# An RWKV block and a cross-attention block in one kernel: group norm and gate taken per quarter, a front with second buffers, waits by chunk, and the bonus sum in four column groups

## The chip, the core and the metric

The kernel runs on one core of a Trainium2 chip. The core has TensorE (PE), VectorE (DVE), ScalarE (ACT), GpSimd (POOL) and SyncE (SP), and 16 DMA engines. The metric is the device time of one execution in microseconds (us); lower is better. All data is float32, and a float32 matmul shows in the trace as two passes, so its counts are twice those of the code.

## The reference

The input `x` is 16 batches of 128 positions by 512 channels; `ctx` has the same shape.

```python
# block 0 (RWKV, state = ctx), H = 32 heads of S = 16
xa = layer_norm(x); sx = previous position of xa - xa
xxx = tanh((xa + sx * maa_x) @ maa_w1)            # five low-rank parts of 32
xk, xw, xv, xr, xg = xa + sx * (maa_stack[j] + xxx[j] @ maa_w2[j])
w = exp(-exp(time_decay + tanh(xw @ td_w1) @ td_w2))
r, k, v = xr @ Wr.T, xk @ Wk.T, xv @ Wv.T;  g = silu(xg @ Wg.T)
for t: a = k_t v_t^T;  out_t = r_t (u * a + s);  s = a + w_t * s
og = group_norm(out) per head * gn_w + gn_b       # mean, variance over the 16 of a head
x1 = x + (og * g) @ Wo.T
xc = layer_norm(x1), shifted and mixed again
x2 = x1 + sigmoid(xr2 @ Wfr.T) * (relu(xk2 @ Wfk.T)**2 @ Wfv.T)
# block 1: instance norms of x2 and ctx, 1x1 convolutions, softmax attention, residual add
```

The term with `u` is called the bonus here: for one position it is `sum_i(r_i * u_i * k_i)` of a head, times `v`.

## The kernel before, in words

The 16 batches go in four quarters of four batches. Each engine runs its own program, and in each the order of the work is a string written out by hand (`ORDER_PE`, `ORDER_DVE` and so on), which says how many steps of which stream come next. An engine executes strictly in that order. The streams are:

- **a** (and **p**): the first stage, by quarter. Load x, layer norm, four turns (transposes) on PE, `EXT` (the normed input with one more column for the shift), `SX` (the difference), `first_mix` into `M1`, the low-rank product and tanh, copies of its rows by DMA (LT<-LE), then five mixes in the order v, w, k, r, g. A mix is two pairs of PE products (L1381) into two PSUM banks, for each of four chunks a `scalar_tensor_tensor` in PSUM (L1033) and an add into `M1` or `M2` (L1030). **p** projects the mixes (L1318), copies the result into `STG` (L778) and stores it in DRAM. The v parts are stored by five DMAs a chunk from ACT's queue (L786, L788). The gate g is `tanh` on ACT and a multiply on DVE (`gate`), and is stored too.
- **scan**: 64 steps, four a batch. SP loads 1 MB of v rows into `VB` (L499), POOL multiplies twice and adds once (L695, L699, L704), ACT writes two start columns (L847, L849) and the decays (L853), DVE runs the recurrence (L1150) and multiplies by r (L1030 on VB), and PE sums over channels in four column groups of 32 (L1440).
- **end**, once a batch: PE sums the bonus (L1454) with the 128-column weights `HEADU` and `HEAD`, DVE adds it to the scan's sum in `OT`; ACT squares `OT`, PE sums the squares (L1462), ACT copies the variance into `GV` (L878), POOL finds its inverse root in 13 small instructions (`newton`) and spreads it into `GS` (L716), PE broadcasts it (L1467), DVE multiplies `OT` by it, SP stores it.
- **c**: the rest of block 0 by quarter. ACT scales by `gn_w` and adds `gn_b` (`affine`, L884), DVE multiplies by the gate (`gated`), then four products of 16 matmuls each (wo, fk, fr, fv), layer norm, turns and mixes.
- **l, l1, l2, l3**: the attention of block 1 in four lanes of batches.

PE waits as whole tiles: `project` waits until all four chunks of a mix are added, `turn_a` until all four batches are normed. Streams a and c share `EXT`, `SX`, `M1`, `M2` and `XN`.

```python
def project(q, f, m):
    w.wait_ge(v_mad, 20 * q + 4 * (f + 1))
def shift_a(q):
    w.wait_ge(v_mad, 20 * q)
def first_mix(q):
    w.wait_ge(p_prj, 20 * (q - 1) + 16 if q else 0)
```

## Time and profile before

| | |
|---|---|
| median of 3 runs | 1023.35 us (1020.78 to 1023.88) |
| the profiled execution | 1016.36 us, its span 1014.6 us |
| busy in the span | PE 896.1, DVE 691.5, POOL 536.5, ACT 396.5 us |
| mean granted clock of PE | 0.936 of full speed |
| first and last scan sum (L1440) | 144.5 and 777.0 us |

A busy engine is not always an engine at full speed: where the granted clock is below 1, PE's passes take up to twice as long. An idle time matters only where nothing else could have ended the kernel later.

### The profile page before, as it was taken

The page shows a single profiled execution, that of the slowest core. Times are in us where ns is not written, and L with a number is a line of the kernel's source. Part 1 is how long each engine was busy: PE and PEld are TensorE (multiplying, and loading weights), DVE is VectorE, ACT ScalarE, POOL GpSimd, SP SyncE. Part 2 cuts the span into 40 slices and gives each one's busy share as a digit, 9 for nine tenths or more (in the row PEclk, how much of TensorE's full clock was granted, in tenths as well). Part 3 has the DMA queues.
Part 4 walks back from the last instruction along what each step waited for, and adds up shares of the span by engine and source line. Part 5 has one row for each costly group of instructions (what it writes and reads, how often), then busy time and mean ns, then how long its engine had stood idle before and what let it go on. Part 6 is the DMA issues. An engine that isn't in the chain of part 4 may idle for free.

```text
span 1014.6 us, 10745 instructions
## 1 busy us (share of the span) xinstructions
PE 896.1 (88%) x3588; PEld 398.5 (39%) x3588; DVE 691.5 (68%) x907; ACT 396.5 (39%) x819; POOL 536.5 (53%) x573
## 2 busy tenths in 40 slices
PE   1679978799786899688998999899998999979998
PEld 1233433343322343243343444344443454444454
DVE  6234499789988687888887698988998224442342
ACT  2013412333212241133223254565355554465395
POOL 2000388669987749648886778889682101000010
PEclk9687997899977899698999999999999999999999
DMA  7351679969689877878979844779642022001001
GB/s 270 134 125 73 179 178 222 233 171 233 162 187 216 209 184 196 212 145 224 243 182 281 216 112 100 183 192 227 163 99 83 21 73 83 21 4 39 21 0 42
DMA packets 100089, 150.69 MB, mean 149 GB/s; under 512 B 22850, under 2 KB 64066, under 8 KB 91842
## 3 DMA queue, kind: packets, MB, share of 16 engines
q1 hardware_dynamic: 73410, 129.03, 50.4%
q10 hardware_dynamic: 26624, 20.98, 8.5%
q8 instruction: 28, 0.46, 0.2%
q14 instruction: 27, 0.22, 0.1%
HBM read 115.38 MB, written 33.55 MB: 147 GB/s over the span
## 4 chain that ended last, share of the span: by engine, by line
PE 59%; DVE 14%; POOL 12%; issue 6%; ACT 5%; ACTq 2%; DMA 2%; SPq 0%; POOLq 0%; DVEq 0%
PE PS L1318 38%; PE PS L1381 4%; PE PS L1543 4%; POOL VB L704 4%; PE PS L1440 3%; PE PS L1520 2%; DVE PS L1033 2%; PE PS L1325 2%; POOL VB L699 2%; DVE VB L1150 2%; DVE M L1030 2%; DVE VB L1030 2%; POOL VB L695 2%; DVE M L1033 2%; PE PS L1454 1%
## 5 line engine op out<-in xcount | busy, mean ns | idle before, releaser
L1318 PE MATMUL PS<-M,W 128*128 128x512 f32 x672 | 329.8, 634 | 23.7 <-DVE M L1033 12.3
L1318 PEld LDWEIGHTS PS<-M,W 128*128 128x128 f32 x672 | 128.7, 202 | 198.2 <-issue 167.5
L704 POOL TENSOR_TENSOR VB<-VB 128x1024 f32<-128x1024 f32 x64 | 151.4, 2366 | 58.9 <-ACT VB L849 56.2
L1150 DVE TENSOR_TENSOR_SCAN VB<-PS,VB 128x512 f32<-128x512 f32 x128 | 149.1, 1206 | 25.9 <-POOL VB L704 17.3
L587 POOL TENSOR_SCALAR NM<-MV 128x2 f32<-128x2 f32 (+1 forms) x24 | 6.2, 258 | 283.7 <-DVE MV L1278 183.0
L1030 DVE TENSOR_TENSOR VB<-VB,PS 128x2048 f32<-128x2048 f32 x64 | 145.9, 2280 | 1.5
L695 POOL TENSOR_TENSOR VB<-KR,VB 128x1008 f32<-128x1008 f32 x64 | 129.7, 2026 | 17.5 <-DMA VB<-scr_vs 17.5
L699 POOL TENSOR_TENSOR VB<-WG,VB 128x1008 f32<-128x1008 f32 x64 | 129.3, 2020 | 0.0
L1033 DVE SCALAR_TENSOR_TENSOR PS<-PS,VEC,SX 128x512 f32<-128x512 f32 x80 | 60.2, 752 | 87.7 <-PE PS L1381 72.4
L1318 PE MATMUL PS<-W,M 128*128 128x512 f32 x224 | 105.1, 595 | 0.0
L1296 DVE TENSOR_REDUCE SM<-PS 128x1 f32<-128x512 f32 x64 | 44.0, 688 | 58.9 <-PE PS L1543 58.4
L1440 PE MATMUL PS<-VB,HEAD 128*32 128x512 f32 x512 | 72.5, 643 | 12.3 <-DVE VB L1030 7.0
L778 ACT ACTIVATE STG<-PS 128x512 f32<-128x512 f32 x48 | 28.5, 594 | 122.3 <-PE PS L1318 110.6
L1381 PE MATMUL PS<-LE,W 32*128 32x512 f32 x64 | 47.7, 834 | 29.0 <-DVE M L1030 21.1
L853 ACT ACTIVATE PS<-WP 128x512 f32<-128x512 f32 x64 | 38.3, 598 | 80.4 <-DVE VB L1150 74.1
L1318 PE MATMUL PS<-W,SX 128*128 128x512 f32 x128 | 61.1, 597 | 0.0
L1543 PE MATMUL PS<-LS 128*128 128x512 f32 x112 | 58.6, 617 | 1.6 <-ACT LE L973 1.6
L1318 PEld LDWEIGHTS PS<-W,M 128*128 128x128 f32 x224 | 40.5, 190 | 44.0 <-issue 43.2
L1030 DVE TENSOR_TENSOR M<-PS,EXT 128x512 f32<-128x512 f32 x80 | 55.2, 690 | 2.3
L973 ACT ACTIVATE LE<-PS,SM 128x512 f32<-128x512 f32 x44 | 30.1, 684 | 53.1 <-DVE SM L1296 53.1
L1381 PE MATMUL PS<-LT,W 32*128 32x512 f32 x64 | 48.2, 841 | 0.0
L1033 DVE SCALAR_TENSOR_TENSOR LS<-PS,WOB,X 128x512 f32<-128x512 f32 x14 | 10.4, 748 | 46.0 <-PE PS L1318 46.0
(167 smaller groups left out, 1280.5 us busy)
## 6 DMA issues: line engine op xcount, KB each, us to landing
VB<-scr_vs SPq DMA_DIRECT2D x64, 1024.0 KB, 7.9
W<-in_w SPq DMA_DIRECT2D x8, 1024.0 KB, 9.8
X<-in_x SPq DMA_DIRECT2D x4, 1024.0 KB, 8.2
scr_vs<-STG ACTq DMA_DIRECT2D x64, 64.0 KB, 5.7
scr_v<-STG ACTq DMA_DIRECT2D x16, 256.0 KB, 6.9
scr_w<-STG ACTq DMA_DIRECT2D x16, 256.0 KB, 8.3
scr_k<-STG ACTq DMA_DIRECT2D x16, 256.0 KB, 2.7
KR<-scr_k SPq DMA_DIRECT2D x16, 256.0 KB, 8.1
```

The source lines that it names most:

```text
L695: po.tensor_tensor(vo, KO[:, 0:N2 - 1].unsqueeze(1).to_broadcast([P, S, N2 - 1]), vo, ALU.mult).then_inc(g_kv, 1)
L699: po.tensor_tensor(ve, KE[:, 0:N2 - 1].unsqueeze(1).to_broadcast([P, S, N2 - 1]), ve, ALU.mult).then_inc(g_kv, 1)
L704: po.tensor_tensor(flat(bv[:, 0]), flat(bv[:, 0]), flat(bv[:, 1]), ALU.add).then_inc(g_kv, 1)
L853: ac.activation(PS[:, 5, :].rearrange("p (j n) -> p j n", n=N2), WP[:, bb % 2, m].unsqueeze(1).to_broadcast([P, 8, N2]), ACT.Copy).then_in ...
L1030: return dv.tensor_tensor(o, a, b, op)
L1033: return dv.scalar_tensor_tensor(out=o, in0=a, scalar=s, in1=b, op0=op0, op1=op1)
L1150: sc = dv.tensor_tensor_scan(s_, PS[:, 5, :], b_, 0.0, ALU.mult, ALU.add)
L1296: dv.reduce_max(SM[:, cs, tc, 0:1], PS[:, BANK_L[bb, ("sc", tc)], :], AX_X, negate=True).then_inc(vb[ln], 1)
L1318: mm = pe.matmul(o, l, r, start=i == 0, stop=i == 3)
L1381: mm = pe.matmul(PS[:, ns[i], :], W2[DM * g:DM * g + DM, 2 * i + j, :], low_rank(f, i), start=True, stop=True)
L1440: mm = pe.matmul(PS[32 * g:32 * g + 32, 4, :], HEAD[:, m, 0], VB[:, k % NB, :, 4 * g:4 * g + 4].rearrange("p s j n -> p j s n"), start=m = ...
L1543: pe.matmul(PS[:, n, :], X[:, 2, tc * P:(tc + 1) * P], X[:, 3, :], start=True, stop=True).then_inc(pb[ln], 1)
```

## The change

1. **Norm and gate by quarter.** Squares, variance, inverse root and scaling leave stream `end` and are done once a quarter at the head of stream `c`. The inverse root works on 128 columns, four times, instead of on 32 columns, 16 times. `affine` and `gated` go; DVE's new `normed` does 12 instructions a quarter. The gate is stored as half the projection (an ACT copy), and its tanh and product come in stream c.
2. **Bonus in four column groups.** 32 small matmuls a batch with 32-column weights, four ACT copies into the block-diagonal `DG`, one matmul that broadcasts 192 columns.
3. **Front ahead.** Odd quarters have their own `EXT` and `SX` (in space of `LL` and `LS`), and the front is a stream of its own beside the mixes (stream `m`). In the first quarter the mixes of v, w and k have four PSUM banks instead of two.
4. **Waits by chunk.** PE waits for each chunk or pair of chunks just before the matmul that reads it. The add of a mix takes two chunks at once (but for g).
5. **Queues.** The v stores go from ACT's queue to SP's. ACT's second start column goes; POOL's add leaves the first column out.
6. All five order strings are new.

```diff
-                    for wt, cols in ((HEADU, slice(0, L)), (HEAD, slice(L, L + N2))):
+                    w.wait_ge(a_dg, 4 * bb)
+                    w.wait_ge(v_ot, 4 * bb - 1 if bb else 0)
+                    for wt, at, n, to in ((HEADU, 0, 32, 192), (HEAD, L, 16, 224)):
                         for m in range(C4):
-                            mm = pe.matmul(PS[:, 7, cols], flat(wt[:, m]), RQ[:, m, cols], start=m == 0,
-                                           stop=m == C4 - 1)
+                            for g in range(4):
+                                mm = pe.matmul(PS[H * g:H * g + H, 7, to:to + n], wt[:, m],
+                                               RQ[:, m, at + n * g:at + n * g + n], start=m == 0, stop=m == C4 - 1)
                     mm.then_inc(p_end, 1)
...
+                    w.wait_ge(a_dg, 4 * (bb + 1))
+                    pe.matmul(PS[:, 7, 0:192], SAME[:].rearrange("p g h -> p (g h)"), flat(DG[:]), start=True,
                               stop=True).then_inc(p_end, 1)
...
             def stream_c():
                 for q in range(NQ):
+                    w.wait_ge(a_sq, 4 * (q + 1))
+                    n = banks.take(w, BANK_C[q, "var"], a_gv, q + 1)
+                    for c in range(C4):
+                        for b in range(QB):
+                            mm = pe.matmul(PS[H * b:H * b + H, n, 0:L], SAME[:, 0], SQ(q)[:, c, b * L:(b + 1) * L],
+                                           start=c == 0, stop=c == C4 - 1)
+                    mm.then_inc(p_gn, 1)
+                    w.wait_ge(g_gn, 14 * (q + 1))
+                    pe.matmul(PS[:, n, :], SAME[:].rearrange("p g h -> p (g h)"), SQ(q)[:, 0, :], start=True,
+                              stop=True).then_inc(p_gn, 1)
...
+            def norm_gate(q):
+                for m in range(4):
+                    w.wait_ge(d_og, 16 * (q + 1))
+                    w.wait_ge(v_mad, 10 * NQ)
+                    w.wait_ge(p_fr, 4 * q)
+                    ac.activation(SQ(q)[:, m, :], OG(q)[:, m, :], ACT.Square).then_inc(a_sq, 1)
...
+                ac.activation(GV[:], PS[:, n, 0:L], ACT.Identity, bias=EB[:]).then_inc(a_gv, 1)
+                for m in range(4):
+                    ac.activation(SQ(q)[:, m, :], XN[:, m, :], ACT.Tanh).then_inc(a_gate, 1)
...
+            def normed(q):
+                for m in range(4):
+                    w.wait_ge(p_gn, 2 * q + 2)
+                    stt(O[:, m, :], O[:, m, :], vec(V_GNW + m), PS[:, n, :], ALU.mult, ALU.mult).then_inc(v_scl, 1)
+                for m in range(4):
+                    stt(G[:, m, :], G[:, m, :], 1.0, XN[:, m, :], ALU.add, ALU.mult).then_inc(v_gate, 1)
+                    stt(O[:, m, :], O[:, m, :], vec(V_GNB + m), G[:, m, :], ALU.add, ALU.mult).then_inc(v_y, 1)
...
+            def stream_n():
+                for q in range(NQ):
+                    w.wait_ge(a_gv, q + 1)
+                    yield from newton(GR[:], GV[:], GT[:], g_gn, 14 * q)
+                    po.tensor_tensor(btv(SQ(q)[:, 0, :]), GR[:].unsqueeze(1).to_broadcast([P, 4, L]),
+                                     MASK[:].unsqueeze(2).to_broadcast([P, 4, L]), ALU.mult).then_inc(g_gn, 1)
...
+        EXTS = [EXT[:], LL[:, 3 * E:3 * E + C4 * QB * (L + 1)].rearrange("p (c b t) -> p c b t", c=C4, b=QB)]
+        SXS = [SX[:], LS[:, 1]]
...
-                w.wait_ge(v_mad, 20 * q)
-                yield from shift(v_sub)
+                w.wait_ge(v_mad, 10 * (q - 1))
+                yield from shift(v_sub, q % 2)
...
-                w.wait_ge(v_mad, 20 * q + 4 * (f + 1))
...
+                yield from four_mm(PS[:, n, :], [(W[:, wi, ec, m * P:(m + 1) * P], M[:, ec, :]) for ec in range(C4)], p_prj,
+                                   (w, v_mad, 10 * q + 2 * f, 2))
...
+            def store_v(q, m):
+                w.wait_ge(a_cp, 12 * q + m + 1)
+                for g in range(4):
+                    sp.dma_start(vs_late[q, m, g], rows).then_inc(d_vs[m], 16)
+                sp.dma_start(dr["v"][q, m], STG[:, ss, :]).then_inc(d_st_["v"][m], 16)
...
-                    w.wait_ge(a_s0, 2 * k + 2)
-                    po.tensor_tensor(flat(bv[:, 0]), flat(bv[:, 0]), flat(bv[:, 1]), ALU.add).then_inc(g_kv, 1)
+                    po.tensor_tensor(vo, vo, ve, ALU.add).then_inc(g_kv, 1)
...
-                    w.wait_ge(p_end, 3 * bb + 3)
-                    tt(OT[:], OT[:], PS[:, 7, 3 * L:4 * L].unsqueeze(1).to_broadcast([P, C4, L]), ALU.mult).then_inc(v_ot, 1)
```

## Rows read from the trace of the kernel before

**Rows 1.** The page: busy time of the engines; shares of the last chain

```profile
PE 896.1 (88%) x3588; PEld 398.5 (39%) x3588; DVE 691.5 (68%) x907; ACT 396.5 (39%) x819; POOL 536.5 (53%) x573
...
PE 59%; DVE 14%; POOL 12%; issue 6%; ACT 5%; ACTq 2%; DMA 2%; SPq 0%; POOLq 0%; DVEq 0%
```

**Rows 2.** Busy time by stretch: PE, weight loads, DVE, ACT, POOL, clock, DMA

```profile
0.00:90.00 90.00, 53.99 (x149) 22.37 (x150) 37.31 (x54) 18.00 (x31) 6.53 (x26) 0.79 0.53 161
90.00:200.00 110.00, 93.83 (x359) 39.70 (x358) 79.10 (x93) 30.62 (x65) 65.31 (x52) 0.92 0.79 190
200.00:600.00 400.00, 354.54 (x1559) 148.33 (x1557) 328.93 (x373) 118.68 (x266) 301.36 (x286) 0.91 0.80 197
600.00:777.00 177.00, 169.35 (x786) 78.79 (x786) 158.47 (x204) 95.96 (x203) 145.82 (x156) 0.99 0.66 162
777.00:1014.60 237.60, 224.35 (x746) 109.33 (x738) 87.71 (x187) 133.28 (x257) 17.51 (x55) 0.99 0.12 33
```

**Rows 3.** What PE waited for in the first 90 us: total, times, longest

```profile
PE PS L1325 <- ACT XN L745: 15.4, 1, 15.4
PE PS L1318 <- DVE M L1033: 6.0, 1, 6.0
PE PS L1381 <- DVE M L1030: 5.2, 3, 3.1
PE PS L1381 <- ACT STG L802: 4.2, 1, 4.2
```

**Rows 4.** What PE waited for from 200 to 600 us

```profile
PE PS L1381 <- DVE M L1030: 12.2, 6, 3.4
PE PS L1440 <- DVE VB L1030: 7.0, 4, 4.4
```

**Rows 5.** PE's timeline, 570 to 600 us: start, duration, instructions

```profile
577.59 1.05 PE L1454 MATMUL PS<-RQ,HEADU 128*128 128x128 f32 x8
...
579.32 3.65 PE L1318 MATMUL PS<-W,M 128*128 128x512 f32 x8
...
589.13 0.46 PE L1462 MATMUL PS<-KR,SAME 128*32 128x32 f32 x32
589.52 1.98 PE L1318 MATMUL PS<-W,SX 128*128 128x512 f32 x4
...
597.44 1.07 PE L1440 MATMUL PS<-VB,HEAD 128*32 128x512 f32 x8
```

**Rows 6.** DVE's groups: busy, mean ns, idle before and its releasers

```profile
L1033 DVE SCALAR_TENSOR_TENSOR PS<-PS,VEC,SX 128x512 f32<-128x512 f32 x80 | 60.2, 752 | 87.7 <-PE PS L1381 72.4 <-PE PS L1362 13.3 <-PE PS L1318 2.0
L1030 DVE TENSOR_TENSOR M<-PS,EXT 128x512 f32<-128x512 f32 x80 | 55.2, 690 | 2.3
...
L1030 DVE TENSOR_TENSOR OT<-OT,PS 128x512 f32<-128x512 f32 x32 | 21.7, 679 | 6.7 <-PE PS L1440 4.0 <-PE PS L1467 2.5
L1033 DVE SCALAR_TENSOR_TENSOR STG<-STG,PS 128x512 f32<-128x512 f32 x32 | 21.7, 678 | 18.3 <-PE PS L1318 18.3
L1030 DVE TENSOR_TENSOR SX<-EXT 128x1024 f32<-128x1024 f32 x16 | 19.8, 1273 | 17.3 <-ACT EXT L754 12.0 <-ACT EXT L903 5.2
```

**Rows 7.** POOL's groups

```profile
L704 POOL TENSOR_TENSOR VB<-VB 128x1024 f32<-128x1024 f32 x64 | 151.4, 2366 | 58.9 <-ACT VB L849 56.2
...
L610 POOL TENSOR_TENSOR GT<-GT,GV 128x32 f32<-128x32 f32 x48 | 15.0, 313 | 2.9
...
L716 POOL TENSOR_TENSOR GS<-GR,MASK 128x128 f32<-128x128 f32 x16 | 7.3, 455 | 1.4
...
L602 POOL TENSOR_SCALAR GR<-GV 128x32 int32<-128x32 int32 x16 | 4.3, 268 | 37.6 <-ACT GV L878 37.0
```

**Rows 8.** ACT's timeline, 53 to 56 us, its DMA issues

```profile
53.03 2.64 ACTq L786 DMA_DIRECT2D scr_vs<-STG  x4
55.70 0.62 ACTq L788 DMA_DIRECT2D scr_v<-STG  x1
```

**Rows 9.** ACT's groups

```profile
L849 ACT ACTIVATE VB<-S 128x16 f32<-128x16 f32 x64 | 14.2, 221 | 2.8 <-ACT STG L778 1.5 <-issue 0.8 <-ACT STG L828 0.4
...
L873 ACT ACTIVATE KR<-OT 128x512 f32<-128x512 f32 x16 | 10.0, 625 | 24.7 <-DVE OT L1030 24.7
```

**Rows 10.** What SP's queue waited for

```profile
SPq L499 <- PE PS L1440: 316.5, 52, 18.4
```

More of the change, by code:

```diff
@@ L177 @@
 BANK_A.update({t: 2 + i % 2 for i, t in enumerate(TAKES_P)})
-TAKES_C = [("wo", b) for b in range(4)] + [("tr", ec) for ec in range(4)] + [("fk", f) for f in range(4)]
+for _t in TAKES_A:
+    if _t[0] == "mix":
+        BANK_A[_t] = _t[3] % 2 + (6 if _t[1] == 0 and _t[2] < 3 and _t[3] // 2 else 0)
+TAKES_C = [("var",), ("rstd",)] + [("wo", b) for b in range(4)] + [("tr", ec) for ec in range(4)] + [("fk", f) for f in range(4)]
 TAKES_C += [(n, b) for b in range(4) for n in ("fr", "fv")]
@@ L817, in stream_p @@
                         yield
-                        yield from store(NAMES[0], q, m)
+                    hs, n = slot(("t", q)), BANK_A["td1", q]
+                    w.wait_ge(p_td1, q + 1)
+                    ac.activation(STG[:, hs, 0:NT // 2], PS[:, n, 0:NT // 2], ACT.Tanh).then_inc(a_td, 1)
+                    yield
                     for m in range(4):
@@ L887, in stream_c @@
             def stream_c():
-                for m in range(C4):
-                    affine(0, m)
-                    yield
                 for q in range(NQ):
+                    yield from norm_gate(q)
                     w.wait_ge(g_stc, 4 * (q + 1))
@@ new lines, in stream_a, with stream_m @@
+            def stream_a():
+                for q in range(NQ):
+                    for b in range(QB):
+                        stats_a(q, b)
+                        yield
+                    yield from sums_a(q)
+                    if q == 0:
+                        yield from centre_wv()
+                    yield from shift_a(q)
+                    yield from first_mix(q)
+            def stream_m():
+                for q in range(NQ):
+                    for f in range(5):
+                        yield from mix(q, f)
@@ L1418, in stream_a, with stream_m @@
                         yield from low_a(q, part)
+            def stream_m():
+                for q in range(NQ):
                     for f in range(5):
```

370 lines of the change are left out of this document (171 added, 199 removed), and 170 rows, old and new, of tables (ORDER_ACT, ORDER_DVE, ORDER_PE, ORDER_POOL).

## The prediction

> **What bounds the kernel now.** I read the page first, for the busy shares and the chain that ended last, then PE's, DVE's and POOL's busy time by stretch, then what PE waited for in each stretch, then the groups of each engine for the durations.
>
> PE is busy for 896.1 us of 1014.6, and the last chain runs through it for 59%; DVE has 14% and POOL 12% [rows 1]. But part of the busy time is at a lowered clock. Busy time times what the clock lacks of 1 is 0.21 x 54.0 = 11 us up to 90 us, 0.08 x 93.8 = 8 up to 200, 0.09 x 354.5 = 32 up to 600, and 4 after that, 55 us in all [rows 2]. At full clock PE's work is thus some 896 - 55 = 841 us. The other 1016 - 841 = 175 us of the profiled execution are 118 us of idle PE (36.0, 16.2, 45.5, 7.7 and 13.2 in the five stretches, span minus busy) and those 55; 2 us lie around the span. After 600 us little is left to win; before it, about 98 us of idle and 51 of clock stand [rows 2].
>
> Why is PE idle there? At the start, because the first stage is one serial line: 15.4 us until the first normed tiles, 6.0 for `first_mix`, 5.2 for mix adds that hold both banks, 4.2 for a tanh [rows 3]. From 200 to 600 us, because DVE comes late with adds (12.2) and scan products (7.0) [rows 4], and DVE and POOL are themselves 82% and 75% busy there [rows 2]. POOL's own chain has waits in it that are not work: 56.2 us for ACT's second start column before its add, and 37.0 us for the variance [rows 7].
>
> **The change part by part, PE.** The bonus took 577.59 to 579.32, so 1.73 us a batch for 16 passes; the sum of squares 0.39 us for 32 passes of 32 columns in four groups [rows 5]. The new bonus is 32 passes of 32 columns and 32 of 16. Nothing of 16 columns is in the trace; I take the price of the 32-column ones, 0.39, since they can hardly cost more, and the low bound is half of it. That is 0.8 us. The broadcast grows from 128 to 192 columns, by 0.1 us or so (a 512-column pass is 3.65/8 = 0.46 at most [rows 5]). Per batch 1.73 + 0.39 go and 0.8 + 0.1 come: 1.2 saved, 19 us over 16 batches. Per quarter come 32 passes of 128 columns in four groups, the same columns as one scan sum, 1.07 us [rows 5], and one broadcast of 512 columns, 0.9: 8 us over four. PE's work falls by about 11 us. If small passes would not run side by side, 64 of them at 1.73/16 = 0.11 us are 7 us a batch, so the other bound is +80 us; the row at 589.13 speaks against it, with 12 ns a pass.
>
> The Trainium skill says in "TensorEngine Tiling (Array Packing)", section Instruction Overhead, that a matmul costs about 60 cycles however few columns it has, and warns against taking the tiling factor from a dimension that is already small. By that page 64 passes are an estimated 64 x 25 ns = 1.6 us and the bonus would save almost nothing, so the forecast would be some 13 us higher. The 32 passes in 0.39 us [rows 5] do not fit a price paid one after the other, so I go by the row.
>
> **POOL.** The inverse root took 4.3 + 7.3 us plus four kinds of 48 instructions at about 0.3 us (one row of the four stands), 69 us in all [rows 7]. On 128 columns one instruction should take up to 0.46, as L716 does; the spread to 512 columns lies between that and the 2.37 of 1024, say 1.3. A quarter is 13 x 0.45 + 1.3 = 7 us, all 28. So 40 us of work go, with the 37 us wait in the middle of the scan work, and the 56.2 us wait for ACT goes wholly. POOL's add itself I leave at 2.3. Off the path this is worth nothing; its worth is in the scan products that DVE delivers earlier.
>
> **DVE.** Out go 16 gate products, 16 scalings of `OT` (0.68 each) and 16 `gated`, in come 48 `scalar_tensor_tensor`s at 0.68 to 0.75 [rows 6]: nothing saved, but 32 of them move from the mixes and scans to stream c. 64 adds of 0.69 become 32 double ones; the nearest row is the 1024-element subtraction at 1.27 [rows 6], so 44.2 becomes 41, bounds 38 and 44. It is 3 us.
>
> **ACT and SP.** ACT loses 64 start columns of 0.22, gains 64 copies into `DG` of about the same (0.22, up to 0.3), and the squares (0.625 [rows 9]) only move. What matters is issue time: four v stores took 2.64 us and the fifth 0.62 [rows 8], over 3 us a chunk, 16 chunks, so 52 us leave ACT for SP. The 4.2 us wait for the decay's tanh [rows 3] stood behind such issues and goes. On SP they are queued between loads that wait for scan sums, 316.5 us in 52 waits, 6 us each, at most 18.4 [rows 10]. What is behind such a wait is a v store, and behind that the `STG` slot and ACT's next copy.
>
> **The front.** Of the first 36 us of idle PE I count off 2 to 3 of the 15.4 (transposes follow the norms one by one, and run beside them), 2 of the 6.0, the 5.2 (four banks), 3 for v projections that now start after the first pair, 4.2 for the tanh, and of the 11 us of lowered clock a third, since the clock here follows idle stretches: 20 us, of which I take 15, because the first chain stays serial in its dependences. The second `EXT` and `SX` free the turns and the shift of the next quarter, but `first_mix` still waits until r of the quarter before is projected, as `M1` is single. So the lead is the four projections of g, 16 matmuls of 0.9 or 14 us, and no quarter. From 90 to 200 us I take 8 of 16.2 + 8 us.
>
> **The middle.** From 200 to 600 us idle and clock cost 45.5 + 32 = 77 us. With POOL's waits gone, DVE relieved of 22 us, waits by chunk and the early front, I take just under half, 35. This is the largest term and a judgement: its bounds are 0 (DVE, 82% busy, keeps its pace) and 65.
>
> **What it adds.** Each quarter of stream c now begins with a chain: four squares 2.5, sum 1.1, copy 0.3, inverse root 7, broadcast 0.9, 12 DVE instructions 9, together 21 us, where affine and gated took about 4, woven into the quarter before. It can't begin before the last fr product of the quarter before, since the squares lie in `M2`. That is 17 us more a quarter. While it runs, PE has the attention of the quarter before: from its shapes about 15 columns-of-512 matmuls a batch, 13 us, 52 us a quarter. So it is hidden but for rough edges, 5 us. If the cover is gone it costs 68.
>
> **Sum.** -11 (PE) -15 (front) -8 -35 (middle) +5 = -64, so 1016.4 becomes 952 us in the profiled execution. The median of the runs shown is 7 us above the profiled one; I predict 958 us.
>
> **Rivals.**
> - *Middle at DVE's pace.* The scans still leave DVE no earlier, as it is busy for 328.9 of the 400 us there [rows 2] and its work is unchanged. Then the term of 35 is 0 to 10: 985 us. For it speaks that DVE's share even rises to 158.5 of 177 us after 600 us [rows 2]; against it that DVE's waits are on POOL and PE. The same time comes if v stores sit behind waiting loads on SP (6 waits of 6 us) or if the front's lead is cut by `M1`.
> - *Everything fits.* Middle gives 65: 925 us. PE's 830 us of work plus 25 at the start and 20 at the end would even allow 875, so it is not excluded.
> - *Slower: the norm chain is not covered.* POOL works in order, and its inverse root stands among the scan multiplies; if its input is late, the multiplies behind it wait, then DVE, then PE. The price is the 17 us a quarter and the 7 us that POOL stands in it, 24 or 96 in all, against 69 gained elsewhere: 1023 - 69 + 96 = 1050 us. It decides from the third quarter on in which PE has nothing else in its order during the chain (72 us); in one or two it takes 24 to 48 back.
> - *The column groups don't run side by side.* Plus 80 us, which also ends above 1023. The row of 0.39 us makes it unlikely.
>
> **How the numbers follow.** Forecast with its own range 940 to 975: 0.52. Everything fits: 0.15. Middle at DVE's pace or SP: 0.20, 975 to 1010. No change, within 0.3% (3 us, about what a measurement can tell): 0.04. Slower: 0.09 (chain 0.07, groups 0.02). Below 920 or above 1005 I leave about 0.05 and 0.15, so the range is 918 to 1003. Faster has 0.52 + 0.15 + 0.20 = 0.87.
>
> **What would show it.** In the profile after, PE's busy time should be near 850 or less with a clock of 0.96 or more; PE's idle time before 90 us some 20 instead of 36. L1454's successor should show 64 small passes in about 0.8 us a batch. POOL's idle time before its add should be near nothing, its inverse root 56 instructions at 0.4 to 0.5. The last scan sum should stand at about 710 instead of 777 us. It is wrong if PE waits for `normed` more than 10 us in all, if SP's waits lengthen the copies from `STG`, or if DVE is busy over 92% until the last scan with PE idle beside it.

## The result, and the profile of the kernel after

The changed kernel takes 1046.6 us (1043.3 to 1047.2, 4 runs) against 1023.6 beside it: a ratio of 1.022 [1.020, 1.025], 23 us slower, where 958 us were forecast. The profiled execution took 1046.2 us. Times here and below are medians and ratios are of means, both of undisturbed executions: one of the four of e5 took 4896 us and is left out.

The page of the kernel after, busy times and the shares of the last chain, as in [rows 1]:

```profile
PE 898.5 (86%) x3980; PEld 387.1 (37%) x3980; DVE 708.1 (68%) x875; ACT 394.1 (38%) x807; POOL 505.6 (48%) x403
...
PE 63%; DVE 17%; issue 5%; DMA 5%; ACT 4%; POOL 3%; SPq 2%; ACTq 0%; DVEq 0%; POOLq 0%
```

Busy time by stretch of the kernel after, columns as in [rows 2]:

```profile
0.00:90.00 90.00, 62.93 (x174) 26.57 (x175) 41.25 (x57) 21.26 (x33) 6.54 (x26) 0.89 0.60 170
90.00:200.00 110.00, 94.89 (x422) 35.47 (x421) 80.48 (x82) 28.54 (x64) 66.00 (x38) 0.86 0.85 195
200.00:600.00 400.00, 331.44 (x1640) 130.77 (x1640) 314.49 (x315) 104.95 (x228) 270.24 (x164) 0.88 0.77 189
600.00:777.00 177.00, 160.10 (x839) 71.92 (x838) 151.40 (x192) 87.18 (x185) 122.95 (x105) 0.96 0.64 155
777.00:1044.40 267.40, 249.10 (x911) 122.36 (x909) 120.45 (x231) 152.19 (x297) 39.90 (x72) 0.98 0.15 41
```

Read as in the prediction: what PE's busy time lacks of full clock is 0.11 x 62.9 + 0.14 x 94.9 + 0.12 x 331.4 + 0.04 x 160.1 + 0.02 x 249.1 = 71 us, so its work at full clock is 898.5 - 71 = 827 us, 14 less than before. The work fell as forecast. The rest of the span grew: idle PE is 146 us (27.1, 15.1, 68.6, 16.9, 18.3) instead of 118, the clock's share 71 instead of 55. Most of it is the stretch from 200 to 600 us, 68.6 + 40 against 45.5 + 32 in [rows 2]; after 600 us idle and clock together cost 47 us instead of 25.

What PE waited for in the kernel after, in the first 90 us (first two rows, beside [rows 3]) and from 200 to 600 us (beside [rows 4]):

```profile
PE PS L1341 <- ACT XN L762: 12.1, 4, 11.5
PE PS L1332 <- DVE M L1042: 5.3, 1, 5.3
```

```profile
PE PS L1399 <- DVE M L1039: 13.9, 8, 3.7
PE PS L1461 <- DVE VB L1039: 11.4, 5, 5.7
PE PS L1332 <- DVE M L1042: 10.9, 3, 4.7
PE PS L1332 <- DVE LS L1042: 10.6, 1, 10.6
```

The last row is new: Wo of quarter 0 waits for `normed`. The scan sums wait longer for DVE than before (11.4 against 7.0).

What POOL waited for in the kernel after (its waits for the last layer norms left out), beside the waits at the end of the lines of [rows 7]:

```profile
POOL VB L714 <- DMA VB<-scr_vs: 110.7, 23, 17.5
...
POOL NM L606 <- DVE MV L1249: 43.4, 4, 20.5
POOL WP L704 <- DMA WG<-scr_w: 27.3, 5, 11.3
POOL GR L621 <- ACT GV L893: 25.1, 4, 9.7
```

The wait for ACT's second start column is gone, as forecast. In its place stand 110.7 us of waits for the loads of `VB`, which took 17.5 us before.

The starts of VectorE's scans show where the time goes. Batch 8 starts at 421 us, 27 us *earlier* than before (448). Then the gap from batch 9 to 10 is 66 us (39 before), from 11 to 12 it is 70 (36), from 14 to 15 it is 54 (41), and the last scan sum stands at 846.5 us instead of 777.0. Each of these long gaps holds the norm and gate of a quarter. The first Wo result is added at 529.5 us, 20.6 later than before. The end comes only 30 us later although the last scan sum comes 69.5 later, because 198 us lie behind that sum now and 238 before.

### The profile page after: what moved, and what is told of

Read it like the earlier page. It is cut to its first block, busy times and chain, and to the rows that moved or that the text cites. A ratio compares the mean times of both kernels' runs of the same rounds, so it can differ in the third digit from the quotient of the medians.

```text
span 1044.4 us, 11193 instructions
## 1 busy us (share of the span) xinstructions
PE 898.5 (86%) x3980; PEld 387.1 (37%) x3980; DVE 708.1 (68%) x875; ACT 394.1 (38%) x807; POOL 505.6 (48%) x403
## 4 chain that ended last, share of the span: by engine, by line
PE 63%; DVE 17%; issue 5%; DMA 5%; ACT 4%; POOL 3%; SPq 2%; ACTq 0%; DVEq 0%; POOLq 0%
PE PS L1332 42%; PE PS L1576 5%; PE PS L1399 4%; DVE VB L1154 3%; PE PS L1461 3%; PE PS L1553 3%; PE PS L1341 3%; DVE VB L1039 3%; DVE PS L1042 2%; DVE M L1042 2%; DVE M L1039 2%; DMA scr_v<-STG 2%; DVE SX L1039 1%; PE PS L1544 1%; DVE LS L1042 1%
## 5 line engine op out<-in xcount | busy, mean ns | idle before, releaser
L1332 PE MATMUL PS<-M,W 128*128 128x512 f32 x672 | 338.9, 647 | 24.3 <-DVE M L1042 18.0
L714 POOL TENSOR_TENSOR VB<-KR,VB 128x1008 f32<-128x1008 f32 x64 | 131.2, 2049 | 110.7 <-DMA VB<-scr_vs 110.7
L722 POOL TENSOR_TENSOR VB<-VB 128x1008 f32<-128x1008 f32 x64 | 152.9, 2389 | 4.5
L718 POOL TENSOR_TENSOR VB<-WG,VB 128x1008 f32<-128x1008 f32 x64 | 131.5, 2054 | 0.0
L1461 PE MATMUL PS<-VB,HEAD 128*32 128x512 f32 x512 | 74.7, 665 | 13.0 <-DVE VB L1039 12.8
L1399 PE MATMUL PS<-LL,W 32*128 32x512 f32 x128 | 47.7, 839 | 24.2 <-DVE M L1039 19.5
L1042 DVE SCALAR_TENSOR_TENSOR PS<-PS,VEC,SX 128x512 f32<-128x512 f32 x40 | 28.9, 752 | 51.1 <-PE PS L1399 41.3
L982 ACT ACTIVATE LL<-PS,SM 128x512 f32<-128x512 f32 x44 | 30.1, 684 | 59.3 <-DVE SM L1307 59.2
L1042 DVE SCALAR_TENSOR_TENSOR PS<-PS,VEC,LS 128x512 f32<-128x512 f32 x40 | 29.1, 753 | 28.4 <-PE PS L1399 25.2
L1332 PE MATMUL PS<-LL,LS 128*128 128x512 f32 x88 | 41.5, 603 | 3.5 <-ACT LL L1028 3.5
L1341 PE MATMUL PS<-ID,XN 128*128 128x128 f32 x128 | 23.0, 299 | 21.1 <-ACT XN L762 12.1
```

The lines of the kernel that those rows point to most:

```text
L714: po.tensor_tensor(vo, KO[:, 0:N2 - 1].unsqueeze(1).to_broadcast([P, S, N2 - 1]), vo, ALU.mult).then_inc(g_kv, 1)
L718: po.tensor_tensor(ve, KE[:, 0:N2 - 1].unsqueeze(1).to_broadcast([P, S, N2 - 1]), ve, ALU.mult).then_inc(g_kv, 1)
L722: po.tensor_tensor(vo, vo, ve, ALU.add).then_inc(g_kv, 1)
L1042: return dv.scalar_tensor_tensor(out=o, in0=a, scalar=s, in1=b, op0=op0, op1=op1)
L1332: mm = pe.matmul(o, l, r, start=i == 0, stop=i == 3)
L1341: mm = pe.transpose(PS[:, n, i * P:(i + 1) * P], tile, ID[:])
```

## The experiments

Ratios are to the kernel before on the same chip; the changed kernel's own is 1.022 [1.020, 1.025]. The changed kernel was not run again on the chips of the experiments, where the kernel before took 1017 to 1020 us (median), and executions of one kernel there differ by up to 1.3% (e13: 1014.3 to 1027.9). So two ratios that differ by half a per cent or less are not told apart. "Last sum" is the start of the last scan sum in the kept trace: 846.5 us in the changed kernel, 777.0 before.

### Where v and g are stored, and the waits by pair

First theory (A): the v stores, now in SP's queue between loads, hold the loads. `e1_v_on_act` puts them back on ScalarE, `e3_vg_on_act` g as well, `e2_loads_between` keeps them on SP and moves loads ahead of them. `e4_whole_waits` undoes the wait by pairs of chunks in the projections.

```diff
# e1 (in copy_a's loop for v, ScalarE; SP's five issues a chunk go)
+                        ss = SLOT_STG["v", q, m]
+                        w.wait_ge(a_cp, 12 * q + m + 1)
+                        for g in range(4):
+                            rows = STG[32 * g:32 * g + 32, ss, :].rearrange("h (s n) -> h s n", n=N2)
+                            ac.dma_start(vs_late[q, m, g], rows).then_inc(d_vs[m], 16)
+                        ac.dma_start(dr["v"][q, m], STG[:, ss, :]).then_inc(d_st_["v"][m], 16)
# e4
-                                   (w, v_mad, 10 * q + 2 * f, 2))
+                                   (w, v_mad, 10 * q + 2 * f + 1, 4))
```

Expected of e1: 

> The changed kernel, but the five v stores of a chunk are issued from ACT's queue right behind the copy, and SP's steps for them do nothing. Theory A (the v stores on SP hold back the VB loads behind them, so POOL waits 110.7 us for VB<-scr_vs where it waited 17.5, and the last scan sum comes at 846 us instead of 777): POOL's wait for that DMA falls below 50 us, the last scan sum comes before 800 us, the time falls from 1046.6 to 990 to 1020 us. Theory B (the new orders, the norm chain and DVE's slow all-SBUF instructions cost it, the loads are only late because the scans are): the wait may move but the time stays within 8 us of 1046, or rises, as ACT gets 52 us of issue time back.

Expected of e2: 

> The changed kernel with SP's order alone altered: in the second, third and fourth quarter the next KR, WG and VB loads stand ahead of the burst of v stores or between its chunks; the stores stay on SP. Theory A: about half of what moving them to ACT gives, 1020 to 1035 us, since a load and a store still hold each other up in one queue. Theory B: no change, 1040 to 1050 us.

Expected of e3: 

> As the v stores on ACT, and the stores of the gate too, which stood on SP in the kernel before as well. SP waited 40.7 us in 7 times for the gate's copies in the changed kernel. Theory A: loads behind them come earlier, another 3 to 10 us below the run with the v stores alone. Rival: the gate's stores fall where no VB slot is free, and it is within 3 us of that run. Theory B: as for the first, no gain over 1046.

Expected of e4: 

> The changed kernel with one part undone: a projection waits for all four chunks of its mix before its first matmul instead of pair by pair. If the wait by chunk gives what I forecast (3 us at the start and part of the middle), this is 3 to 12 us slower than 1046.6. If waits by chunk do harm by stalling PE inside an open group, it is faster. If DVE's pace sets the mixes anyway, within 3 us.

Measured: e1 1062.1 us, 1.044 [1.040, 1.048]; e2 1094.1 us, 1.075 [1.070, 1.079]; e3 1059.7 us, 1.042 [1.039, 1.044]; e4 1058.8 us, 1.041 [1.038, 1.043]. Theory A fell: stores on SP are some 20 us better than on ScalarE. With the stores on ScalarE GpSimd still waits 115.6 us for the loads of `VB` (110.7 in the changed kernel, under 50 expected), and the last sum stands at 861.4 us. Letting loads pass the stores is worse still: in e2 ScalarE waits longer for the `STG` slots (49.4 us at L829 on scr_v, 21.8 in the changed kernel) and GpSimd longer for loads (150.2 us); which of the two makes the time was not tested. Undoing the waits by pair costs about 18 us, more than the 3 to 12 expected.

### The products of norm and gate beside GpSimd's multiplies

VectorE's timeline of the kernel after, `normed` of quarter 0 (start, duration, instructions), and then GpSimd's and TensorE's beside it:

```profile
506.38 2.73 DVE L1042 SCALAR_TENSOR_TENSOR LS<-LS,VEC,PS 128x512 f32<-128x512 f32 x4 [4.62 <-PE PS L1505]
509.02 0.69 DVE L1042 SCALAR_TENSOR_TENSOR LS<-LS,XN 128x512 f32<-128x512 f32 x1
509.74 2.72 DVE L1042 SCALAR_TENSOR_TENSOR LS<-LS,VEC 128x512 f32<-128x512 f32 x1
512.38 2.48 DVE L1042 SCALAR_TENSOR_TENSOR LS<-LS,XN 128x512 f32<-128x512 f32 x1
...
522.31 0.68 DVE L1042 SCALAR_TENSOR_TENSOR LS<-LS,XN 128x512 f32<-128x512 f32 x1
523.03 0.75 DVE L1042 SCALAR_TENSOR_TENSOR LS<-LS,VEC 128x512 f32<-128x512 f32 x1
```

```profile
506.90 2.00 POOL L718 TENSOR_TENSOR VB<-WG,VB 128x1008 f32<-128x1008 f32 x1
...
514.27 2.44 POOL L718 TENSOR_TENSOR VB<-WG,VB 128x1008 f32<-128x1008 f32 x1
...
541.74 0.23 POOL L606 TENSOR_SCALAR NM<-MV 128x4 f32<-128x4 f32 x1 [19.90 <-DVE MV L1249]
```

```profile
523.83 15.95 PE L1332 MATMUL PS<-W,LS 128*128 128x512 f32 x32 [10.55 <-DVE LS L1042]
```

The four products with an operand in PSUM take 0.68 us each. Those with both tensor operands in SBUF take 2.4 to 2.8 us as long as GpSimd multiplies beside them, and 0.68 to 0.75 once it stands (from 521.8 us on). One exception, the product at 509.02, began with GpSimd's add of 508.98: it took 0.69, and the add 2.92 instead of 2.39. GpSimd's multiplies go from 2.00 to 2.44 us in the same stretch. So `normed` took 17.4 us instead of 9, and PE stood 10.55 us for it.

The Trainium skill has the rule, in "SBUF — State Buffer", section Who interferes with whom: a VectorE instruction with two SBUF inputs contends with a GpSimd instruction that reads SBUF, and whichever comes first holds the shared port for its whole instruction. The trace agrees for VectorE: 0.7 us become 0.7 plus most of one GpSimd multiply of 2.0. GpSimd loses less, 0.44 us a multiply. The prediction did not weigh it, though the trace of the kernel before shows it: a product with both tensor operands in SBUF that takes 0.69 us as a rule took up to 2.81 there (min, median and max in ns):

```profile
L1033 DVE SCALAR_TENSOR_TENSOR X<-STG,X x16: 675/691/2814, 569.9 to 970.9; 128x512 f32<-128x512 f32 x16
```

Three runs tell the theories apart. `e5_psum_products` writes the tanh into PSUM and keeps the gate product there, in one bank, so that each tanh now waits for the product before it and no longer for the spread; `e6_no_products` leaves out the gate and the bias product; `e7_short_root` leaves out two Newton steps of three.

```diff
# e5
-                    w.wait_ge(p_gn, 2 * q + 2)
+                    w.wait_ge(a_gv, q + 1)
+                    w.wait_ge(v_y, 4 * q + m)
...
-                    ac.activation(SQ(q)[:, m, :], XN[:, m, :], ACT.Tanh).then_inc(a_gate, 1)
+                    ac.activation(PS[:, n, :], XN[:, m, :], ACT.Tanh).then_inc(a_gate, 1)
...
-                    stt(G[:, m, :], G[:, m, :], 1.0, XN[:, m, :], ALU.add, ALU.mult).then_inc(v_gate, 1)
+                    stt(G, G, 1.0, XN[:, m, :], ALU.add, ALU.mult).then_inc(v_gate, 1)   # G in PSUM
# e6: both products of a chunk
+                    dv.tensor_copy(O[:, m, 0:1], G[:, m, 0:1]).then_inc(v_y, 1)
# e7
-                for i in range(3):
+                for i in range(1):
```

Expected of e5: 

> The whole computation, but the gate's tanh is written to the PSUM bank that the mean square has left, and the gate product stays there, so that of the 12 products of a quarter none has all its operands in SBUF. Theory C (the chain of norm and gate is slow because VectorE's products with all operands in SBUF take 2.0 to 2.8 us beside GpSimd's scan multiplies instead of 0.7): each of the 8 falls to about 0.75 us, 10 to 13 us less for each quarter that lies in the scan stage, less some 4 us because one tanh now waits for the product before it; over three quarters 18 to 27 us, so 1020 to 1028 us and a ratio to the kernel before of 1.00. Theory D (the time is lost where GpSimd and VectorE, in order, stand at stream c's steps with the scans queued behind them, whatever the products cost): the products get short, but the scan's end moves by under 8 us, ratio 1.015 to 1.02.

Expected of e6: 

> Leaves out the gate product and the bias product (8 of the 12 of a quarter); a copy of one column takes the place of each pair. Upper bound of what the products cost. Theory C: 15 us a quarter on VectorE and on the way to the projection Wo, of which three quarters lie in the scan stage: 30 to 45 us, ratio 0.98 to 0.995. Theory D: under 12 us, ratio 1.01 or more.

Expected of e7: 

> Leaves out two of the three Newton steps of the inverse root (8 of 14 GpSimd instructions of a quarter, 0.3 to 0.5 us each, 3.8 us a quarter). If the chain square, sum, root, spread, products is uncovered (the rival of the prediction), each of the first three quarters gets 3.8 us shorter and GpSimd has as much more for the scan: 8 to 12 us less, ratio 1.011 to 1.014. If it is covered, nothing: ratio 1.022.

VectorE's timeline of e5 at the same place:

```profile
506.50 0.69 DVE L1043 SCALAR_TENSOR_TENSOR PS<-PS,XN 128x512 f32<-128x512 f32 x1
507.23 0.75 DVE L1043 SCALAR_TENSOR_TENSOR LS<-LS,VEC,PS 128x512 f32<-128x512 f32 x1
508.65 0.70 DVE L1043 SCALAR_TENSOR_TENSOR PS<-PS,XN 128x512 f32<-128x512 f32 x1 [0.67 <-ACT PS L899]
```

Every product is back at 0.69 to 0.75 us, and GpSimd's multiplies at 2.00, so the contention is shown as the cause of their length. `normed` takes 10.6 us instead of 17.4, PE's wait for it is gone, the first Wo result is added at 520.8 us instead of 529.5, and the last sum stands at 839.0. In its place PE waits 3.8 us for a copy that stands behind the tanhs in ScalarE's order. Yet e5 took 1045.2 us (1036.5 to 1046.9), 1.024 [1.017, 1.031]: nothing of the 10 us of idle PE can be seen at the end, though by the interval a gain of half a per cent is not excluded. e6 took 1020.9 us, 1.003 [1.000, 1.006], some 20 us less than the changed kernel, with the last sum at 820.6. e7 took 1035.3 us, 1.017 [1.012, 1.021], between the two answers expected of it. By theory C the run e5 should have come near e6; it did not. The length of the products is real, but only part of their price.

### The places where the queues stand

`e8_pool_scans_first`: GpSimd stood 19.9 us (521.8 to 541.7, row above) at the second layer norm of quarter 0 with scan multiplies queued behind; this run puts four scan steps ahead of it. `e9_squares_early`: ScalarE stood 12.0 us for the squares of quarter 0, whose buffer is now the second `SX` of the odd quarters; this run puts them elsewhere. `e10_chain_early` also moves mean, spread and root ahead in the orders; `e11_early_psum` adds e5 to that. `e12_scan_between` moves one scan sum, one load and three scan steps ahead of stream c's block.

```diff
# e8, GpSimd's order
-    n:2 scan:1 n:12 scan:9 c:4 scan:4 c:1 scan:8
+    n:2 scan:1 n:12 scan:13 c:5 scan:8
# e9, squares of quarter 0 by chunk into LE
-                    w.wait_ge(v_mad, 10 * NQ)
+                    if q:
+                        w.wait_ge(v_mad, 10 * NQ)
+                    else:
+                        w.wait_ge(p_mix, 10 * NQ - 2)
+                        w.wait_ge(p_sq, m - 1)
# e12, TensorE's order
-    c:49 l:8 scan:1 end:1
+    c:16 scan:1 c:33 l:8 end:1
```

Expected of e8: 

> Nothing is changed but GpSimd's order at one place: the four small instructions of the second layer norm of quarter 0, for which GpSimd waited 19.9 us (521.8 to 541.7) with scan multiplies behind them, go behind the next four scan steps. Theory D: about 9 us of scan work fill the wait, the scan's end comes 5 to 9 us sooner, ratio 1.013 to 1.017. Theory C: the scans gained wait for VectorE anyway, which is busy with the slow products and then waits for Wo; ratio 1.02 to 1.025.

Expected of e9: 

> The whole computation. Only the squares of quarter 0 go to another place (by chunk into two free rows of the first stage's low rank buffer) instead of LS, which the front of the odd quarters now uses as its second buffer; so ScalarE no longer waits 12.0 us (477.6 to 489.6) for the last double add of quarter 3 with its scan and project steps queued behind. No order is changed. Theory E (the second buffers hold the first norm chain and, through ScalarE's order, the scan): the 12 us go, part comes back as ScalarE's wait for TensorE's mean of squares, which stands later in TensorE's order; first use of Wo 3 to 6 us sooner, ratio to the kernel before 1.015 to 1.02. Rival (the wait is covered, since the chain waits for TensorE's order anyway): no change, 1.022 to 1.024.

Expected of e10: 

> As the kernel before this one, and three steps of the chain of quarter 0 stand earlier in the orders: TensorE's mean of squares ahead of the last two mixes of quarter 3, its spread where the mean stood, GpSimd's root ahead of two scan multiplies. Theory E: the chain square, mean, root, spread, products starts about 12 us sooner and its first use of Wo about 8 us sooner, 6 to 9 us less than the changed kernel: ratio 1.014 to 1.017. Rival: VectorE, with four scan steps ahead of the products, gives nothing of it on: 1.020 or more.

Expected of e11: 

> Both together: the earlier chain of quarter 0, and the gate's tanh and product in PSUM in all quarters, so that no product beside GpSimd's multiplies has all operands in SBUF. If the two causes add, Wo of quarter 0 starts 15 us sooner than in the changed kernel: ratio 1.005 to 1.012. If a third cause (scans held behind stream c's block on TensorE and on the queues) sets the end, 1.015 to 1.02.

Expected of e12: 

> Only orders: one scan step of TensorE goes from behind its block of 49 steps of stream c (fk, fr, fv of quarter 0, 562.3 to 605.2, whole 43 us) to behind the first 16 of them; one load of SyncE goes ahead of the stores and loads of stream c, and three scan steps of GpSimd ahead of the inverse root of quarter 1. The product that this scan sum reads was made at 567.7 and summed at 611.0; the next load stood until 612.1 and GpSimd and VectorE ran out of scan work. Theory F (in the changed kernel the scans starve behind TensorE's block, which keeps TensorE busy now and idle later): the gap between the scan starts of batches 11 and 12 falls from 70 us to 58 to 62, the last scan sum comes 8 to 12 us sooner, ratio 1.010 to 1.015. Rival (the later stages are paced by TensorE's own work, the scans only wait with it): the gap falls but the end stays, 1.020 to 1.024.

Measured: e8 1043.6 us, 1.023 [1.018, 1.029]; e9 1041.3 us, 1.024 [1.019, 1.029]; e10 1047.8 us, 1.030 [1.025, 1.035]; e11 1035.6 us, 1.019 [1.015, 1.023]; e12 1043.4 us, 1.026 [1.022, 1.030]. None of e8, e9 and e12 is faster than the changed kernel's 1.022, and e10 is slower (1.030). e11 differs from e10 by e5's products alone and is 1.1% faster, with intervals that do not meet: with the chain early, the length of the products does reach the end. Against the changed kernel e11's 1.019 is not told apart. The traces show what becomes of the time. First ScalarE's timeline at the squares, of the kernel after:

```profile
489.63 1.15 ACT L886 ACTIVATE LS<-LS 128x512 f32<-128x512 f32 x2 [12.00 <-DVE M L1039]
```

and of e9:

```profile
478.68 1.15 ACT L893 ACTIVATE LL<-LS 128x512 f32<-128x512 f32 x2 [7.41 <-DMA LS<-scr_o]
...
483.77 1.15 ACT L893 ACTIVATE LL<-LS 128x512 f32<-128x512 f32 x2 [3.45 <-PE PS L1507]
```

The wait for the double add is gone, and behind it stood two others, the load of o and PE's mean. In e10 the mean comes earlier still (copied at 478.5 us against 485.5 in e9), but VectorE then waits 12.4 us for TensorE before the last mixes, `normed` begins only at 503.3, and Wo of quarter 0 is added at 530.0 instead of e9's 523.2.

SyncE's timeline of the kernel after in the gap between batches 11 and 12:

```profile
565.42 0.64 SPq L518 DMA_DIRECT2D VB<-scr_vs  x1
589.24 0.32 SPq L427 DMA_DIRECT2D scr_g<-STG  x1
589.74 0.37 SPq L545 DMA_DIRECT2D XN<-scr_g  x1
590.21 0.52 SPq L549 DMA_DIRECT2D M<-scr_o  x1
612.13 0.52 SPq L518 DMA_DIRECT2D VB<-scr_vs  x1
```

No load of `VB` is issued for 46.7 us, because TensorE's 49 steps of stream c (busy from 562.3 to 605.2) stand ahead of the scan sum that frees a buffer. TensorE's timeline of e12 shows that sum moved, and the next one:

```profile
571.86 1.07 PE L1461 MATMUL PS<-VB,HEAD 128*32 128x512 f32 x8
...
610.66 3.53 PE L1461 MATMUL PS<-VB,HEAD 128*32 128x512 f32 x16
```

The gap of 70 us became 71, with the next sum now the one that stands. Theory F is refuted for a single step: moving one sum only made the next one the late one.

### Both kernels without norm and gate

The pair that decides. Both kernels lose norm and gate whole; a copy of one column stands for each output chunk, and every order, load and store stays.

```diff
# e13, changed kernel: squares, mean, root, spread, tanh and products go
+                for m in range(4):
+                    w.wait_ge(d_og, 16 * (q + 1))
+                    w.wait_ge(d_gl, 16 * (q + 1))
+                    dv.tensor_copy(O[:, m, 0:1], XN[:, m, 0:1]).then_inc(v_y, 1)
# e14, kernel before: squares, sum, root, spread, last product by batch, gate product, affine go
-                    mm.then_inc(p_end, 1)
+                    mm.then_inc(p_end, 3)
```

Expected of e13: 

> The changed kernel without the norm and the gate: no squares, mean, inverse root, spread, tanh or products; a copy of one column stands in for each output chunk, all orders, buffers, loads and stores stay. If theory G holds (the rest of the change gives what was forecast, 25 to 45 us, and the norm and gate by quarter cost far more than the 5 us of the forecast because they are not covered), this is far under the changed kernel, 970 to 995 us, a ratio to the kernel before of 0.955 to 0.975, and 20 us or more under the kernel before treated in the same way (next run). If theory H holds (the rest of the change loses too, by its orders and its longer in-order queues), it stands within 10 us of the kernel before treated in the same way.

Expected of e14: 

> The kernel before without its norm and gate: no square, sum, root, spread and last product by batch, no gate product in the projection, no affine step; a copy of one column for each output chunk. What it gives is the price of norm and gate in the kernel before. Both theories expect little, since GpSimd's roots and VectorE's products there lie beside TensorE's work: 15 to 30 us less than the kernel before, ratio 0.97 to 0.985. The difference to the run before this one is the worth of everything else in the change.

Measured: e13 1021.9 us, 1.004 [1.001, 1.007]; e14 1022.1 us, 1.002 [1.000, 1.005]. Theory H holds for the gain: without norm and gate the two kernels are equal within 0.2%, so all the rest of the change together, forecast at 69 us, is worth nothing. Norm and gate cost the changed kernel 1.8% (1.022 to 1.004), 18 us, and the kernel before nothing. e6 had that already (1.003): once eight products a quarter are gone, leaving out squares, mean, root, spread and tanh as well gives nothing more. These are prices by removal, and they do not add up: undoing the store queue (e1) or the waits by pair (e4) costs the changed kernel about 2% each, so if those hold without the norm too, something else in the change must lose about as much. The last sum hints at the order strings, 816.9 us in e13 against 783.8 in e14, but no run has the new orders alone.

Why leaving so much out gives the kernel before nothing is in its waits. GpSimd's waits from 100 to 500 us in e14:

```profile
POOL VB L704 <- ACT VB L841: 72.5, 12, 10.7
POOL VB L695 <- DMA VB<-scr_vs: 41.0, 12, 10.7
```

In the kernel before itself these two were 38.4 and 14.8 us there, and 26.4 us went to the variance. The root's 60 us of work and that wait are gone, and the time comes back as longer waits at the next two places. The changed kernel has for the same stretch:

```profile
POOL VB L714 <- DMA VB<-scr_vs: 82.5, 16, 17.5
```

The stretch from 200 to 600 us, first e13, then e14 (e13's kept trace is of its fastest execution, 1014.3 us, e14's of one of 1022.9):

```profile
200.00:600.00 400.00, 332.10 (x1724) 131.36 (x1722) 310.07 (x330) 111.13 (x244) 264.97 (x157) 0.92 0.80 194
```

```profile
200.00:600.00 400.00, 347.20 (x1212) 141.91 (x1210) 325.39 (x349) 104.55 (x235) 261.61 (x154) 0.90 0.78 194
```

Over the whole of e14's trace PE's work at full clock is 829 us, 12 less than before, and idle and lowered clock together 192 us, 18 more.

### Are the loads the pace?

`e17_after_half_loads` and `e18_before_half_loads` cut each `VB` load from the fifth on to its first half; the other half keeps what lay there.

```diff
+                        part = slice(0, S * L if k < NB else S * L // 2)
-                        sp.dma_start(VB[:, k % NB].rearrange("p s j n -> p (s j n)"), src).then_inc(d_vb[k % NB], 16)
+                        sp.dma_start(VB[:, k % NB].rearrange("p s j n -> p (s j n)")[:, part],
+                                     src[:, :, part]).then_inc(d_vb[k % NB], 16)
```

Expected of e17: 

> The changed kernel with every load of the scan's values from the fifth on cut to its first half (the other half of the buffer keeps what lay there); all instructions and waits stay. Theory L (with norm and gate gone from the scan stage and the start columns on ScalarE, the scan is paced by the round of the four buffers: a load of 9.7 us, then GpSimd's three multiplies, VectorE's scan and product, TensorE's sum, and only then the next load; GpSimd's waits for loads grew from 14.8 us to 82.5 us between 100 and 500 us): a load falls to 5 to 6 us, about 4 us less in a round of four chunks, 1 us a chunk, 30 to 60 us less over the scan, ratio to the kernel before 0.965 to 0.99. Rival (TensorE's and VectorE's own order sets the pace and GpSimd's waits for loads are slack): under 10 us, ratio 1.012 or more.

Expected of e18: 

> The same cut of the loads in the kernel before. There GpSimd waits only 14.8 us for loads between 100 and 500 us, so by theory L it gains less than the changed kernel: 0 to 15 us, ratio 0.985 to 1.0. If it gains as much as the changed kernel does, the loads were its pace too, and the change had nothing to win in GpSimd's other waits. If neither gains, the round of the buffers is no bound in either.

Measured: e17 1054.8 us, 1.035 [1.031, 1.039]; e18 1013.4 us, 0.994 [0.992, 0.996]. A load fell from 9.7 to 5.5 us in e17 and from 7.9 to about 5.2 in e18, but theory L fell: with loads half as long the kernel before gains 0.6%, and the changed one loses 1.2%. GpSimd's wait for loads in e17 is still 60.0 us between 100 and 500. The last sum moved 9 us later in e17. A part of the loss may lie in the products. VectorE's groups in `normed` of quarter 1 (600 to 650 us), of the kernel after and then of e17:

```profile
L1042 DVE SCALAR_TENSOR_TENSOR M<-M,VEC 128x512 f32<-128x512 f32 x4 | 6.2, 1560 | 0.1
L1042 DVE SCALAR_TENSOR_TENSOR M<-M,XN 128x512 f32<-128x512 f32 x4 | 4.4, 1106 | 0.9 <-ACT M L898 0.9
```

```profile
L1044 DVE SCALAR_TENSOR_TENSOR M<-M,XN 128x512 f32<-128x512 f32 x4 | 9.2, 2303 | 0.0
L1044 DVE SCALAR_TENSOR_TENSOR M<-M,VEC 128x512 f32<-128x512 f32 x4 | 8.5, 2129 | 0.1
```

In the changed kernel GpSimd stood 2.4 and 1.2 us for loads within this `normed`, in e17 0.6 us in all, and the eight products take 17.7 us instead of 10.6. That these 7 us reach the end is not shown (e5's did not), and the other 6 us were not traced.

### Attempts at a better version

`e15_psum_root2` has e5's products, e9's squares and two Newton steps; `e16_psum_pow` has one power instruction for the whole root.

```diff
# e16
-                    yield from newton(GR[:], GV[:], GT[:], g_gn, 14 * q)
+                    po.tensor_tensor(GR[:], GV[:], HALF[:, 0:1].to_broadcast([P, L]), ALU.pow).then_inc(g_gn, 13)
```

Expected of e15: 

> An attempt at a better version: the squares of quarter 0 out of the second buffer (orders untouched), tanh and gate product in PSUM, and two Newton steps instead of three. If the three gains add: 5 and 3 us from the first two, 3 from the root, ratio 1.010 to 1.018. If the scans' starvation behind stream c sets the end whatever the chain costs: 1.02.

Expected of e16: 

> As the run before this one, but the whole inverse root is one power instruction of GpSimd on 128 x 128 instead of 13 or 9 small ones. No row shows one of this size: on two columns it takes 0.72 us, on four about the same. If it goes by columns at little more than an ordinary operation (0.4 us), the root falls from 6.5 us to under 2 and the ratio to 1.005 to 1.015; if a power costs some 0.1 us a column it takes over 10 us and the run is slower than the one before this one, 1.02 to 1.03.

Measured: e15 1040.2 us, 1.021 [1.017, 1.025], no better than its parts; e16 1098.5 us, 1.079 [1.076, 1.082]. GpSimd's group in e16:

```profile
L732 POOL TENSOR_TENSOR GR<-GV,HALF 128x128 f32<-128x128 f32 x4 | 83.0, 20748 | 15.6 <-ACT GV L903 15.6
```

The power takes 20.7 us a quarter, against about 4.2 for e15's nine small instructions: 66 us more on GpSimd, of which 58 stand in the time. So time added there reaches the end nearly whole; whether through the root itself or through the scan multiplies behind it, the run does not tell. Time taken out there gave less: e7 spared 3.8 us a quarter and came out half a per cent lower, at the edge of what is told apart. The price of the power could have been read beforehand: the expectation took two and four columns for about the same, but the trace has 0.77 us for two and 1.04 for four. No version with the computation kept beat the kernel before; the best was e11 at 1.019.

## Why the prediction was wrong

**PE's work (-11): right.** It fell by 14 us. The bonus passes of the kernel after, groups with busy time, mean ns and waits:

```profile
L1485 PE MATMUL PS<-DG,SAME 128*128 128x192 f32 x32 | 8.7, 352 | 2.9 <-ACT DG L878 2.9
L1479 PE MATMUL PS<-RQ,HEAD 128*32 128x16 f32 x512 | 7.9, 190 | 0.0
L1479 PE MATMUL PS<-RQ,HEADU 128*32 128x32 f32 x512 | 7.8, 204 | 1.5 <-DVE RQ L1039 1.5
```

At 507.1 us the 32 passes of 32 columns were followed 0.27 us later by those of 16, and these 0.66 us later by the next matmul, which had 0.19 us of wait in it: 0.7 us a batch, forecast 0.8. The rival of column groups that don't run side by side is refuted. The prediction's estimate of 1.6 us by the Trainium skill's "TensorEngine Tiling (Array Packing)", section Instruction Overhead, was too high here; it took the page's 60 cycles for all 64 passes one after the other, and they ran in four groups side by side.

**The front (-15): right.** Idle PE before 90 us fell from 36.0 to 27.1 us and the clock's share from 11 to 7: 13 us. The tanh's wait fell from 4.2 to 0.6, the 5.2 of [rows 3] are gone and the first wait is 12.1 instead of 15.4; new are 3.4 us for the decay's exponential (L829) and 4.7 us in which PE waited for nothing that the profile shows. From 90 to 200 us (-8) nothing was won and 4 us were lost: 15.1 + 13.3 against 16.2 + 8. So at 200 us the changed kernel was some 9 us ahead, and not 23.

**GpSimd: its work right, its worth wrong.** Root and spread fell by 43 us (68.7 to 25.2; forecast 40), GpSimd's work as a whole by 31 (536.5 to 505.6), partly because its scan instructions took 9 us longer; the wait for ACT went. The root's instructions took 0.30 to 0.50 on average and the spread 1.04, against 0.45 and 1.3 in the forecast. But "its worth is in the scan products that DVE delivers earlier" failed: GpSimd now waits 110.7 us for loads, whose buffers are freed by scan sums that come no sooner.

**The middle (-35): this is the step that failed.** It was +31, 66 of the 94 us between the forecast of -64 and the +30 of the profiled executions. I took half of the idle time that one engine's waits seemed to cause as winnable, and judged it from that engine's side. e14 shows on the kernel before itself that GpSimd's root and its wait, VectorE's 48 products and TensorE's passes for the norm can all go without any gain; e18 shows nearly the same for the loads. After 600 us, where the forecast had only the chain's 5 us, idle and clock grew by 22. My own rival "middle at DVE's pace" has the right sign but not the size or the mechanism: VectorE was busy for only 314 of the 400 us.

**The norm chain (+5): wrong, it is not covered.** From the copy of the mean to the last product, forecast at 17 us of the 21, it took 30.3, 27.9, 21.9 and 17.2 us in the four quarters: the sizes hold where GpSimd no longer scans, and in the scan they don't. Two prices were missing: the products beside GpSimd (17.4 us in quarter 0, 8.3 in quarter 3) and the buffer. The squares of quarter 0 use `LS`, which is the second `SX` now, so they waited for the last double add. The price of norm and gate by removal is 18 us, but neither missing price accounts for it alone: with the products short (e5) or the buffer free (e9) the time stayed.

**The slower rival** named the mechanism (GpSimd in order, the root among scan multiplies, then VectorE, then TensorE) and its 1050 us is close to the 1047. But the closeness is chance: its gain elsewhere was 69 us (measured: none) and its chain 96 us (measured: 18). A chance of 0.07 for it was far too low.

**Its own signs.** Its sum gives 952 + 7 = 959 us, not 958, which changes nothing. It called itself wrong if PE waited for `normed` more than 10 us in all: PE waited 10.6 us in quarter 0 alone. PE's busy time was to be near 850 us at a clock of 0.96 and was 898.5 at 0.918; its idle time before 90 us 20, and was 27; the last scan sum at 710, and was 846.5. The small passes, GpSimd's idle time before its add (4.5 us) and the root's durations came out as written.

**What stays open.** What paces both kernels from 200 to 600 us, with root, norm, gate or half of each load gone, was not isolated. Each engine works through a fixed order and waits for others at many small places; single places moved one by one (e8 to e10, e12) gave nothing. That the orders as a whole are the bound is only argued: the new order strings were never run without the rest of the change, nor the rest with the old ones.

## What to carry to other kernels

An engine's waits are not a sum to be won where five in-order queues feed each other through a ring of buffers: before forecasting a gain from relief, leave the work out of the kernel as it is, which here took one run (e14) and would have said 0 for norm and gate. Work gathered from many small, woven steps into one chain per quarter must be priced as latency in the path, with every queue that it blocks, unless the cover is ordered beside it. A reused buffer is also a wait: look up who last uses it before calling it free.

## What the runs showed of the hardware

- VectorE's product of 512 columns with both tensor operands in SBUF takes 0.68 to 0.75 us alone and 2.4 to 2.8 beside GpSimd's multiplies, which take 2.44 instead of 2.00 meanwhile. With one operand in PSUM it stays at 0.69 to 0.75 beside the same multiplies, which then take 2.00 (e5).
- 32 matmul passes of 32 columns in four column groups were issued within 0.27 us, 8 ns apiece (507.13 us in the kernel after); the 32 of 16 columns behind them took no less.
- GpSimd's power goes by columns: 0.77 us on 2, 1.04 on 4, 20.7 on 128, about 0.16 us a column, while a multiply on 128 columns takes 0.4 to 0.5.
